# A one-core four-layer transformer kernel: the ends of its index stage are rebuilt

## The reference, cut to what matters

```python
x = L0_attn_x                                   # 1 x 1024 x 512, fp32
x = x + L0_attn(layernorm(x))                   # 128-wide attention
x = x + L0_ffn(layernorm(x))                    # 512 -> 1792 -> 512
x = x + L1_attn(layernorm(x))                   # below
x = x + L1_ffn(layernorm(x))                    # x @ (W + LoRA) + bias

def L0_ffn(h):      # W1, W2, W3 = base + mean|w - base| * sign(w - base)
    return (silu(h @ W1.T) * (h @ W3.T)) @ W2.T

def L1_attn(h):     # 32 heads, 192 q_rank, 64 kv_rank, 128 nope + 64 rope
    q_lat = rmsnorm(h @ q_a_w, q_a_norm_w);  ckv = h @ kv_a_w
    iq = (h @ idx_wq_w).reshape(1, 1024, 16, 128)      # 16 index heads
    ik = h @ idx_wk_w                                  # 1024 x 128
    iw = h @ idx_weights_w * 16 ** -0.5
    idx = einsum('bqn,bnqk->bqk', iw, relu(einsum('bqnd,bkd->bnqk', iq, ik))) * 128 ** -0.5
    mask = causal & (the 128 largest of idx in each row)
    # 32 heads: softmax over the masked scores, values, o_w
```

## Time and profile before

| | |
|---|---|
| runs | 1559.79, 1560.31, 1561.89 us |
| median | 1560.31 us |
| the profiled execution | 1560.82 us, of which 1558.9 us are the span of the trace |
| busy, share of the span | PE 1348.8 us (87%), DVE 1146.0 us (74%), ACT 827.5 us (53%), POOL 655.3 us (42%) |
| FFN's last two groups | 409.48 to 420.52 us |
| end of the FFN to the first index scores | 420.52 to 471.25 us |
| index steps without and with top-k rounds, before pair 0's step | 472.33 to 572.47 us |
| steps 21 (its sums) to 47 | 572.47 to 744.84 us |
| tail, to the first rotated query | 744.84 to 812.70 us |

### The profile page before, as it was taken

The page is one execution under the profiler, slowest core; times in us unless marked ns, Lnnn a source line. Parts: engine busy times, 40 slices in busy tenths (PEclk is TensorE's granted clock), DMA queues, the critical chain, the costliest instruction groups (busy, mean ns, idle before and its releaser), DMA issues.

```text
span 1558.9 us, 21230 instructions
## 1 busy us (share of the span) xinstructions
PE 1348.8 (87%) x7142; PEld 1123.2 (72%) x7142; DVE 1146.0 (74%) x2233; ACT 827.5 (53%) x1794; POOL 655.3 (42%) x620
## 2 busy tenths in 40 slices
PE   2875899999778898779465999999999999999977
PEld 1753688888677876667244888888888888888866
DVE  5544433323438899789987999998888998889864
ACT  3575322223225665566333777667766667667741
POOL 3433000000027664555333655555555555666612
PEclk9966799999989999999566999999999999999998
DMA  6543000000021135545650000000000000000011
GB/s 217 170 154 117 0 1 0 1 1 1 11 85 57 53 104 161 161 133 149 201 173 30 12 1 26 26 26 26 26 27 26 26 26 26 26 26 15 12 64 54
DMA packets 83723, 95.59 MB, mean 61 GB/s; under 512 B 11681, under 2 KB 59297, under 8 KB 83105
## 3 DMA queue, kind: packets, MB, share of 16 engines
q1 hardware_dynamic: 83616, 94.24, 19.3%
HBM read 75.34 MB, written 18.87 MB: 60 GB/s over the span
## 4 chain that ended last, share of the span: by engine, by line
PE 65%; DVE 13%; issue 3%; ACT 2%; POOL 2%; DMA 2%; SPq 2%; DVEq 1%; POOLq 0%; ACTq 0%
PE ps L311 15%; PE ps L313 15%; PE ps L312 15%; PE ps L1561 8%; PE ps L1581 3%; PE ps L1580 3%; DVE xn_l L1238 2%; DVE rop L1196 2%; DMA wuvo<-pr_hl 1%; DVE rop L1194 1%; DVE acc L1173 1%; PE ps L1352 1%; DVE pm L1226 1%; PE ps L1473 1%; DVE rop L1195 1%
## 5 line engine op out<-in xcount | busy, mean ns | idle before, releaser
L652 POOL TENSOR_SCALAR pm<-pm,smx 128x128 f32<-128x128 f32 (+7 forms) x256 | 190.2, 752 | 212.1 <-DVE smx L1232 212.1
L899 ACT ACTIVATE pm<-pm,smx 128x128 f32<-128x128 f32 (+7 forms) x256 | 197.2, 772 | 35.1 <-DVE smx L1226 33.4
L1226 DVE CUSTOM_DVE_ANT_0 pm<-ps,mbias 128x128 f32<-128x128 f32 (+7 forms) x256 | 191.5, 753 | 29.1 <-PE ps L313 14.1
L1561 PE MATMUL ps<-ident,pm 128*128 128x128 f32 x1152 | 174.9, 277 | 10.4 <-DVE xn_l L1238 4.9
L905 ACT ACTIVATE xn_h<-ps 128x512 fp32r<-128x512 f32 (+3 forms) x256 | 129.0, 513 | 85.6 <-PE ps L1561 82.7
L1238 DVE TENSOR_TENSOR xn_l<-ps,xn_h 128x512 fp32r<-128x512 f32 (+3 forms) x256 | 144.6, 587 | 26.6 <-ACT xn_h L905 25.7
L311 PE MATMUL ps<-latT_l,qc_h 128*128 128x512 f32 (+3 forms) x384 | 142.6, 371 | 21.5 <-POOLq L302 12.1
L1561 PEld LDWEIGHTS ps<-ident,pm 128*128 128x128 f32 x1152 | 132.0, 141 | 36.7 <-issue 13.3
L1173 DVE SCALAR_TENSOR_TENSOR acc<-relu,iw,acc 128x768 f32<-128x768 f32 (+4 forms) x105 | 119.1, 1175 | 27.0 <-ACT relu L821 26.4
L313 PE MATMUL ps<-latT_h,qc_h 128*128 128x512 f32 (+3 forms) x384 | 134.1, 349 | 0.0
L312 PE MATMUL ps<-latT_h,qc_l 128*128 128x512 f32 (+3 forms) x384 | 133.7, 348 | 0.0
(11 more groups left out here) (248 smaller groups left out, 3815.0 us busy)
## 6 DMA issues: line engine op xcount, KB each, us to landing
iwq_raw<-in_L_attn_idx_wq_w SPq DMA_DIRECT2D x48, 256.0 KB, 3.2
ow_raw<-in_L_attn_o_w SPq DMA_DIRECT2D x16, 512.0 KB, 4.0
wuvo<-pr_hl SPq DMA_DIRECT2D x16, 512.0 KB, 3.5
base<-in_L_ffn_mean_w SPq DMA_DIRECT2D x28, 256.0 KB, 3.0
wring<-in_L_ffn_w SPq DMA_DIRECT2D x24, 256.0 KB, 3.3
wq<-pr_hl SPq DMA_DIRECT2D x16, 256.0 KB, 2.4
wuvo_h<-wuvo SPq DMA_DIRECT2D x16, 256.0 KB, 2.7
wuvo_l<-wuvo SPq DMA_DIRECT2D x16, 256.0 KB, 3.1
```

Source lines behind the costliest of these rows:

```text
L652: pool.tensor_scalar(pm[:, i % 4, 0:w], pm[:, i % 4, 0:w], smx[:, 32 + i:33 + i], 0.0, ALU.mult, ALU.add).then_inc(hd_p, 1)
L899: act.activation(pm[:, i % 4, 0:w], pm[:, i % 4, 0:w], ACT.Exp, bias=smx[:, i:i + 1], scale=-1.0, accum_out=smx[:, 16 + i:17 + i]).then_in ...
L1226: dve.tensor_tensor_reduce(out=pm[:, i % 4, 0:w], in0=two_banks(2 * (i % 2), w), in1=mbias[:, TRI[t]:TRI[t + 1]], scale=1.0, scalar=3.0 * BIG,
L1561: done = pe.transpose(ps[:, 4 + i % 2, tile(k)], pm[:, tq % 4, tile(4 * c + k)], ident[:])
```

## The change

At the FFN's end the last two groups are worked tile by tile (group 12, then group 13, of a tile), with tile i in bank i; DVE adds and takes statistics as the tiles come. The norm is made in two halves of four tiles, with a square root each (`half_norm`), and PE's and ACT's orders are written out (NORM_ORDER, NORM_EVICT; T is a tile's transpose, L its latent product, R the second square root). ACT runs a square root on a dummy tile first. The barrier is gone. The latent weights are loaded once all gate and up products are made, the key weights once all down products are. `index_weights_hi(0)` stands ahead of the eviction of the keys.

Pairs are worked in the steps 21 to 44, ten in the loop and six in the tail. There are two buffers for the high and low parts, the space of `wf_h` for even pairs and `pr_hl` for odd ones. ACT gathers a pair's result one step later, ahead of that step's relus, and writes the high part behind them; POOL's split is two steps later; SP stores a pair two steps later than before, and loads pair 0 at its step 19 instead of 20. The loads of the final layer's weights are taken one by one, from SP's step 24 on.

```diff
...
-PAIR_AT = {22: 0, 24: 1, 27: 2, 29: 3, 32: 4, 34: 5, 37: 6, 39: 7, 42: 8, 44: 9, 47: 10}
+PAIR_AT = {21: 0, 24: 1, 27: 2, 30: 3, 32: 4, 35: 5, 37: 6, 40: 7, 42: 8, 44: 9}
+LATER = len(PAIR_AT)
...
-DOWN_BANKS = (7, 4, 5, 6, 0, 2, 1, 3)
+DOWN_FIRST = (7, 4, 5, 6, 0, 2, 1, 3)
+NORM_ORDER = "T0 T1 T2 L0 T3 L1 L2 T4 T5 L3 T6 L4 T7 L5 L6 L7"
+NORM_EVICT = "T0 T1 T2 L0 T3 L1 R T4 L2 T5 L3 T6 L4 T7 L5 L6 L7"
...
+        pr_even = wf_h[:].rearrange("p k n -> p (k n)").rearrange("p (m n) -> p m n", m=2)
+        pr_buf = (pr_even, pr_hl[:])
...
-            meet(sp, 2)
+            sp.wait_ge(ff_up, 2 * NI)
             for a, w, src in ((0, QR, qa), (QR, KR + ROPE, kva), (QR + KR + ROPE, IDXH, iww)):
                 sp.dma_start(wlat_raw[:, :, a:a + w], src.rearrange("(k p) n -> p k n", p=P)).then_inc(lt_ld, 16)
+            sp.wait_ge(ff_y, NT)
             sp.dma_start(iwq_raw[:, 2], iwk.rearrange("(k p) n -> p k n", p=P)).then_inc(ik_ld, 16)
...
-            def load_final():
-                sp.dma_start(lA_sb[:], lA.rearrange("n r d -> (n r) d")).then_inc(en_ld, 16)
-                for k in range(NK):
-                    sp.dma_start(lB_sb[:, k, :].rearrange("p (n r) -> p n r", n=LORA_N),
-                                 lB[:, tile(k), :].rearrange("n p r -> p n r")).then_inc(en_ld, 16)
-                for n in range(LORA_N):
+            def load_final(part):
+                if part < NK:
...
             def store_pair(j):
                 sp.wait_ge(pr_sp, j + 1)
-                part = f(pr_hl[:])
+                part = f(pr_buf[j % 2])
...
-            for step in range(2, STEPS):
-                load_index(step)
-                if step == 20:
+            for step in range(2, STEPS + 8):
+                if step < STEPS:
+                    load_index(step)
+                if step == 19:
                     sp.wait_ge(lt_lo, NT)
                     load_pair(0)
                 if step - 4 in PAIR_AT:
                     load_pair(PAIR_AT[step - 4] + 1)
-                if step - 6 in PAIR_AT:
-                    store_pair(PAIR_AT[step - 6])
-            store_pair(8)
-            load_pair(10)
-            load_final()
-            store_pair(9)
-            for j in range(10, PAIRS):
+                if step - 8 in PAIR_AT:
+                    store_pair(PAIR_AT[step - 8])
+                if step >= 24:
+                    load_final(step - 24)
+            for j in range(LATER, PAIRS):
                 if j + 1 < PAIRS:
                     load_pair(j + 1)
                 store_pair(j)
                 if j == 12:
-                    sp.wait_ge(pr_st, 48 * 13)
+                    sp.wait_ge(pr_st[0], 48 * 7)
+                    sp.wait_ge(pr_st[1], 48 * 6)
...
             def split_pair(j):
                 pool.wait_ge(pr_ev, j + 1)
-                reach(pool, pr_st, 48 * j)
-                pool.tensor_tensor(pr_hl[:, 1, :], pr_out[:, j % 2, :], f(pr_hl[:, 0, :]), ALU.subtract)\
+                pool.tensor_tensor(pr_buf[j % 2][:, 1, :], pr_out[:, j % 2, :], f(pr_buf[j % 2][:, 0, :]), ALU.subtract)\
...
-                if step in PAIR_AT:
-                    split_pair(PAIR_AT[step])
+                if step - 2 in PAIR_AT:
+                    split_pair(PAIR_AT[step - 2])
             drop_later(2)
             topk_mask(1)
             pool.wait_ge(tk_mask, 5)
             pool.memset(f(wq_l[KR:P, :, 1, :]), 0.0).then_inc(hd_wz, 1)
             pool.wait_ge(hd_wz, 1)
-            for j in range(11, PAIRS):
+            for j in range(LATER, PAIRS):
...
-            meet(act, 2)
-            sqrt(2, NT)
+            act.activation(table[:], ones[:, 0:1], ACT.Sqrt)
+            sqrt(2, 4)
...
+            for step in NORM_EVICT.split():
+                t = int(step[1:] or 0)
+                if step[0] == "T":
+                    act.wait_ge(ln_tr, NT * 2 + t + 1)
+                    act.activation(xn_h[:, :, tile(t)], ps[:, t % 2, :].rearrange("p (k s) -> p k s", k=NK),
+                                   COPY).then_inc(ln_hi, 1)
+                elif step[0] == "L":
+                    act.wait_ge(lt_mm, t + 1)
+                    act.activation(lat[:, t, :], ps[:, 2 + t % 4, 0:LATW], COPY).then_inc(lt_ev, 1)
+                elif step == "R":
+                    sqrt(3, 4, 4)
+            index_weights_hi(0)
...
-                act.activation(pr_out[:, j % 2, 512:1024], ps[:, 7, :], COPY)
-                act.drain()
-                reach(act, pr_sp, j)
-                reach(act, pr_st, 48 * j)
-                act.activation(pr_hl[:, 0, :], pr_out[:, j % 2, :], COPY).then_inc(pr_ev, 1)
-
-            index_weights_hi(0)
...
+                if step - 1 in PAIR_AT:
+                    pair_evict(PAIR_AT[step - 1])
                 if step in PAIR_AT:
-                    if step == 22:
+                    if PAIR_AT[step] == 0:
                         act.wait_ge(pr_z, 1)
                     pair_transposed(PAIR_AT[step])
                 index_relu(step)
                 if step == 3:
-                    sqrt(3, 16)
-                if step in PAIR_AT:
-                    pair_evict(PAIR_AT[step])
-            for j in range(11, PAIRS):
+                    sqrt(4, 16)
+                if step - 1 in PAIR_AT:
+                    pair_hi(PAIR_AT[step - 1])
+            for j in range(LATER, PAIRS):
                 pair_transposed(j)
                 pair_evict(j)
+                pair_hi(j)
+            act.wait_ge(pr_st[0], 48 * PAIRS // 2)
...
-            for i in range(NT):
+            def down_add(i):
                 dve.wait_ge(ff_y, i + 1)
-                dve.tensor_tensor(xt(i), xt(i), ps[:, DOWN_BANKS[i], :], ALU.add).then_inc(ff_x, 1)
-            for t in range(NT):
-                dve.wait_ge(ff_x, t + 1)
-                dve.bn_stats(stats[:, 6 * t:6 * t + 6], xt(t))
-            meet(dve, 2)
-            norm(2, 2)
+                dve.tensor_tensor(xt(i), xt(i), ps[:, i, :], ALU.add).then_inc(ff_x, 1)
+
+            def down_stats(i):
+                dve.wait_ge(ff_x, i + 1)
+                dve.bn_stats(stats[:, 6 * i:6 * i + 6], xt(i))
+
+            def half_norm(k, first):
+                dve.drain()
+                for t in range(first, first + 4):
+                    dve.bn_aggr(mv[:, t, :], stats[:, 6 * t:6 * t + 6])
+                dve.drain()
+                dve.tensor_scalar(rs_var[:, first:first + 4], mv[:, first:first + 4, 1], EPS, None, ALU.add)
+                rsqrt(k, 4, first)
+
+            down_add(0)
+            for i in range(1, 4):
+                down_add(i)
+                down_stats(i - 1)
+            down_stats(3)
+            half_norm(2, 0)
+            norm_scale(2, 0)
+            norm_scale(2, 1)
+            down_add(4)
+            down_add(5)
+            norm_lo(2, 0)
+            norm_scale(2, 2)
+            down_stats(4)
+            down_add(6)
+            norm_lo(2, 1)
+            norm_scale(2, 3)
+            down_stats(5)
+            down_add(7)
+            down_stats(6)
+            norm_lo(2, 2)
+            down_stats(7)
+            half_norm(3, 4)
+            for t in range(4, NT):
+                norm_scale(2, t)
+                norm_lo(2, t - 1)
+            norm_lo(2, NT - 1)
...
-                reach(pe, pr_ev, j)
+                reach(pe, pr_out_w, j)
...
+            for g in range(NI - 2):
+                for i in DOWN_FIRST if g == 0 else range(NT):
                     if g == 0:
-                        if DOWN_BANKS[i] == 6:
+                        if i == 6:
                             pe.wait_ge(ff_w2, NI)
-                        elif DOWN_BANKS[i] < 4:
-                            pe.wait_ge(ff_mul, 2 * (NI - 1) + DOWN_BANKS[i] % 2 + 1)
-                    last = mm3(pe, ps[:, DOWN_BANKS[i], :], hT_h[:, g % 2, tile(i)], hT_l[:, g % 2, tile(i)],
-                               w2_h[:, g % 2, :], w2_l[:, g % 2, :], g == 0, g == NI - 1)
-                    if g == NI - 1:
-                        last.then_inc(ff_y, 1)
-                    elif i == NT - 1:
-                        last.then_inc(fd_mm, 1)
-            meet(pe, 2)
-            for t in range(NT + 2):
-                if t < NT:
+                        elif i < 4:
+                            pe.wait_ge(ff_mul, 2 * (NI - 1) + i % 2 + 1)
+                    last = down(g, i)
+                last.then_inc(fd_mm, 1)
+            for i in range(NT):
+                down(NI - 2, i)
+                down(NI - 1, i).then_inc(ff_y, 1)
+            for step in NORM_ORDER.split():
+                t = int(step[1:])
+                if step[0] == "T":
                     norm_tile(2, t)
-                if t == 2:
-                    pe.wait_ge(lt_w, 1)
-                if t >= 2:
-                    pe.wait_ge(ln_lo, NT * 2 + t - 1)
-                    reach(pe, lt_ev, t - 5)
+                else:
+                    if t == 0:
+                        pe.wait_ge(lt_w, 1)
```

(7 more changed lines are left out.)

111 lines of the change are left out of this document (58 added, 53 removed).

## The result

The changed kernel takes 1541.64 us (median of four runs, 1538.07 to 1542.84) where the kernel before takes 1560.05 us (four runs, 1554.98 to 1561.89): a ratio of 0.9883 with a 95% interval of 0.9863 to 0.9903, 15 to 21 us faster. 1551 us was forecast. The sign, and most places, were right; the size was about twice what was said (18.4 us by the medians).

What follows compares the result with a forecast made beforehand. Bound by a chain of short steps at the norm, DVE in the loop, top-k rounds in the tail; -12.5 + 5.2 - 8.6 + 6.3 = -9.6 us gives 1551 us, range 1538 to 1560 us.

Steps and rivals of the forecast that it cites:

- the price of the pairs in the loop: Steps 21 to 47: DVE sums lose 26.4 us to POOL instead of 11.9, at 2.4 us a pair: +14.5 us.
- the FFN: Before the index stage: groups to 11 are the same instructions, so nothing moves: 0 us.
- the clock in the norm: FFN end and norm: PE may hold full clock instead of 0.80; no row for it, so not in the value.
- the tail's +6.3: Last sum to first rotated query: one pair more, its split behind the mask, delays the rest: +6.3 us, 4 to 8.
- The norm: FFN's end to first index scores: earlier transposes -9.0, latent weights' conversion -0.9, `iwq_h` ahead of keys' eviction -2.6: -12.5 us.
- the forecast -9.0: FFN's end: the norm's first transposes start at 422.0 instead of 430.96 us: -9.0 us.
- the bound of -15 us: FFN's end and norm: the best case, if PE without its 10.44 us pause holds the full clock.
- Step 17: Index step 17: SP's earlier `lt_lo` wait delays the load for weights 20, so DVE's sums start late: +5.2 us, 4 to 7.
- rival 2: Step 17 and tail: loads are covered, 5.2 us shrinks to 1, tail gives +1: 1542 us; chance 0.11.
- The loop: Steps 21 to 47: DVE's idle time goes, -23.1 us, pairs' splits cost +14.5 us: -8.6 us.
- Rival 1: Loop: POOL splits during DVE's top-k rounds, a pair costs 1.1 us or less, loop gives -20: 1540 us; chance 0.23.
- Rival 4: Loop: splits cost DVE their full 2.35 us plus 0.45 us, some idle time stays: slower, 1565 to 1568 us; chance 0.09.

Runs made afterwards that it cites:

- `table` alone: The kernel before with only the change's unused 4-byte tile allocated at its place, shifting later buffers by 32 bytes: ratio 0.9983 (0.9970 to 0.9996).

## Why the prediction was wrong in size

The step that failed by most is the price of the pairs in the loop, +14.5 us, which was +8.8. Two terms stood at nothing, the FFN and the clock in the norm, and the tail's +6.3 was +8.5.

**The FFN: not in the sum.** "Before and behind the index stage nothing moves ... the same instructions." The instructions are the same, their data's addresses are not. 3.45 us in the two traces, of which the 700 loads of the stretch are 2.5, and as many come with `table` alone. The other 0.9 us lie ahead of the stretch (it begins at 184.52 and 183.59 us); two executions of the kernel before begin it 2.1 us apart (184.52 and 182.39 us), so they are chance as far as these traces tell.

**The norm: -14.3 for -12.5.** Each step stands where it was put: the first transposes 11.13 us behind the last hT_l (407.50 to 418.63) for 20.01 before (410.95 to 430.96), which is the forecast -9.0 within 0.1. Behind them the way to the first sum is 36.0 us for 41.4, which is 5.4 us less where 3.5 were forecast. The 1.8 us more go with the clock. The forecast left it out of its value, as without a row, and kept it for the bound of -15 us; the granted clock from 422.50 to 454.00 us was 1.00 for 0.80, and TensorE no longer stands still for 10.44 us ahead of that. No run separates the clock from the new order, so that it is the whole of the 1.8 us is argued.

**Step 17: +5.15 for +5.2**, with ACT's wait of 7.47 us in its row, and shown by the kernel that takes it away. The forecast's rival 2, that it would be covered, fell. The rows of before were enough: a wait that costs nothing in one step costs its whole length one step earlier.

**The loop: -14.3 for -8.6.** DVE's idle time of 23.1 us went to nothing, as said. The term that was mis-sized is what the pairs cost DVE through POOL: +14.5 us, with 2.4 us for each of ten pairs; it was +8.8 us (DVE busy 158.08 for 149.24). The sums lost 21.1 us (76.0 less 54.9) where 26.4 were forecast. The 2.4 leant on the row at 577.60 us, the dearest of ten: the same trace has the nine others at 0.5 to 1.1 us. In the changed kernel nine steps' sums meet a split and lose 11.3 us together, where 24 us were forecast for ten (the tenth meets a first sum and takes nothing); a split added to each pair costs 1.1 us. The 17 other steps lose 9.7 us where 2.4 were forecast. So the mechanism was wrong in part, and the number came nearer than its two halves.

What was missed is the weights' low part. By the timelines, it is under way on POOL when a sum begins 17 times in 54 in the changed kernel, and these sums are 14.8 us longer in total than the shortest of their kind; before it was 5 times and 1.2 us. The forecast saw that the splits would move against the sums and not that this work moves too. The kernel that holds it back, and the splits with it, took 13.8 us off the sums, the one that holds the splits alone 6.0 us. Rival 1 named the direction, POOL's work in the rounds, and was given 0.23; its 1540 us is near the measured time by luck, since it wanted -20 us from the loop and nothing from the FFN and the clock.

**The tail: +8.5 for +6.3.** The chain was right to the place: pair 12's transposes were forecast 18.8 us behind the last sum and began at 737.05 us, 18.7 us behind it, and pair 10's split ended at 726.72 + 2.36 = 729.1 us, 10.7 us behind it (11.8 forecast). The missing 2.2 us come behind them. In these two traces most lie at the end, where the final weights and the first query are made. From the end of pair 15's products to the first rotation, before and after:

```profile
795.83:812.70 16.87, 11.24 (x74) 10.30 (x73) 9.37 (x13) 7.66 (x14) 7.16 (x5) 0.89 0.26 85
```

```profile
776.20:794.72 18.52, 13.76 (x74) 12.22 (x73) 2.54 (x5) 7.66 (x14) 7.46 (x5) 0.68 0.28 94
```

The same 74 matmuls take 13.76 instead of 11.24 us, at a granted clock of 0.68 for 0.89, and the stretch is 1.65 us longer where the forecast had it 0.5 us shorter. But the second traces of the two kernels, before and after again, have it alike:

```profile
793.08:810.60 17.52, 12.53 (x74) 11.05 (x73) 9.77 (x13) 7.66 (x14) 7.51 (x5) 0.79 0.25 82
774.67:792.19 17.52, 12.45 (x74) 11.05 (x73) 1.28 (x4) 7.66 (x14) 7.48 (x5) 0.79 0.30 100
```

And their tails still differ by 8.5 us (68.11 and 76.60 us): there it is PE's wait for pair 14's load that is longer, 11.90 us for 9.01, where the forecast kept it at 9.21 us (the first pair of traces has 11.06 us for 9.21). So +8.5 us repeats, but not the place of the missing 2.2 us: the clock at the end is one execution's, and the cause stays open.

Rival 4, the slower one, needed 1.2 us a pair more than 2.4; the nine steps lost 1.3 us each. The range held the time, but the forecast's own 1546 to 1556 us did not.
